# Cross-attention and mixture-of-experts kernel: the store of each turned probability block issued from ScalarE, its loads from SyncE, three block buffers

## What is computed

```python
x = x + xattn(ctx, layernorm(x), mask)      # 16 heads of 64; keys and values: context rows and latent rows
#   q = lat @ Wq;  k, v = [ctx, lat] @ Wk, Wv
#   alphas = softmax(mask(q k^T / 8));  out = (alphas v) @ Wo
x = x + ffn(layernorm(x))                   # 8 experts, the best 2 per token, and a shared expert
#   gates: sigmoid(x gate_w), top 2, normalised; h = silu(x w1) * (x w3); y = (h w2) * gate, summed
```

## Time and profile before

| | before |
|---|---|
| median of 3 runs | 1154.0 us |
| profiled execution, its own time | 1153.85 us |
| span of that execution in the trace | 1152.1 us |
| TensorE busy with matmuls | 1083.4 us (94%) |
| TensorE busy with weight loads | 941.8 us (82%) |
| VectorE busy | 926.4 us (80%) |
| ScalarE busy | 792.1 us (69%) |
| GpSimd busy | 615.2 us (53%) |
| first and last matmul of L860 | 41.2 and 1122.4 us |

### The profile page before, as it was taken

The page is one execution under the profiler, slowest core; times in us unless marked ns, Lnnn a source line. Parts: engine busy times, 40 slices in busy tenths (PEclk is TensorE's granted clock), DMA queues, the critical chain, the costliest instruction groups (busy, mean ns, idle before and its releaser), DMA issues.

```text
span 1152.1 us, 28179 instructions
## 1 busy us (share of the span) xinstructions
PE 1083.4 (94%) x7720; PEld 941.8 (82%) x7720; DVE 926.4 (80%) x4095; ACT 792.1 (69%) x2924; POOL 615.2 (53%) x717
## 2 busy tenths in 40 slices
PE   6899999999999999999999999999999999999976
PEld 6788887888888788888888888888888888888755
DVE  3878887888887788888888888778888788888756
ACT  4887777776777677777776677776777776777631
POOL 5555555555555455555555555555555555554421
PEclk9999999999999999999999999999999999999979
DMA  5455455555455555455555555555455555545531
GB/s 153 141 165 155 152 169 161 163 153 154 150 170 155 162 147 159 145 172 161 171 155 154 154 158 170 168 152 149 137 168 168 168 151 154 155 149 163 157 117 33
DMA packets 248717, 176.81 MB, mean 153 GB/s; under 512 B 29424, under 2 KB 215408, under 8 KB 248560
## 3 DMA queue, kind: packets, MB, share of 16 engines
q1 hardware_dynamic: 247376, 173.96, 50.8%
q10 hardware_dynamic: 1184, 1.05, 0.3%
HBM read 103.35 MB, written 71.56 MB: 152 GB/s over the span
## 4 chain that ended last, share of the span: by engine, by line
SPq 26%; PE 24%; DVE 21%; DMA 11%; issue 11%; ACT 5%; POOL 0%; DVEq 0%; POOLq 0%; ACTq 0%
SPq L335 13%; DMA pT<-probsT_dram 9%; SPq L363 6%; PE bank L860 5%; PE bank L873 4%; PE bank L815 4%; PE bank L817 3%; PE bank L816 3%; SPq L328 3%; DVE logits L671 3%; DVE probsT L686 3%; ACT probs L557 3%; SPq L369 3%; DVE h L704 2%; DVE g_eq L603 2%
## 5 line engine op out<-in xcount | busy, mean ns | idle before, releaser
L453 POOL TENSOR_TENSOR probs<-probs,rdenom 128x512 f32<-128x512 f32 x256 | 266.4, 1041 | 405.0 <-DVE rdenom L680 400.4
L557 ACT ACTIVATE probs<-logits,neg_max 128x128 f32<-128x128 f32 x1024 | 398.7, 396 | 0.9 <-DVE neg_max L671 0.9
L873 PEld LDWEIGHTS bank<-kvT,tT 128*128 128x128 f32 x2048 | 268.8, 192 | 120.3 <-issue 106.8
L860 PE MATMUL bank<-pT,kv_f 128*128 128x512 f32 x512 | 269.3, 607 | 44.2 <-DMA pT<-probsT_dram 43.9
L873 PE MATMUL bank<-kvT,tT 128*128 128x128 f32 x2048 | 270.7, 275 | 0.0
L716 DVE TENSOR_TENSOR cT_lo<-bank,cT_hi 128x512 fp32r<-128x512 f32 x256 | 175.2, 685 | 83.8 <-ACT cT_hi L527 83.7
L671 DVE CUSTOM_DVE_ANT_0 logits<-bank,mask_add 128x128 f32<-128x128 f32 x1024 | 232.6, 282 | 6.1 <-PE bank L873 5.9
L527 ACT CAST cT_hi<-bank 128x512 fp32r<-128x512 f32 x256 | 150.0, 586 | 113.1 <-PE bank L860 112.5
L557 ACT ACTIVATION_READ_ACCUMULATOR probs<-logits,neg_max 128x1 f32 x1024 | 197.6, 193 | 0.0
L512 ACT ACTIVATE h_tanh<-bank 128x256 f32<-128x256 f32 x160 | 61.6, 385 | 180.7 <-PE bank L817 178.3
L686 DVE STREAM_TRANSPOSE probsT<-probs 128x512 f32<-128x512 f32 x256 | 176.0, 688 | 0.7 <-issue 0.5
(11 more groups left out here) (102 smaller groups left out, 1996.4 us busy)
## 6 DMA issues: line engine op xcount, KB each, us to landing
probsT_dram<-probsT SPq DMA_DIRECT2D x256, 256.0 KB, 2.4
pT<-probsT_dram SPq DMA_DIRECT2D x1024, 64.0 KB, 2.2
gates<-gates_dram SPq DMA_DIRECT2D x62, 256.0 KB, 4.2
kv_raw<-in_ctx SPq DMA_DIRECT2D x32, 128.0 KB, 2.8
kv_raw<-in_x SPq DMA_DIRECT2D x32, 128.0 KB, 2.9
mask_raw<-in_mask_BxS_ik SPq DMA_DIRECT2D x32, 128.0 KB, 3.4
x_res<-in_x SPq DMA_DIRECT2D x32, 128.0 KB, 2.7
out<-out_sb SPq DMA_DIRECT2D x32, 128.0 KB, 3.0
```

What stands on the lines that cost most here:

```text
L453: nc.gpsimd.tensor_tensor(by_pair, by_pair, rdenom[n][:, :].unsqueeze(2).unsqueeze(3).broadcast_to([P, PAIRS, P // QUAD, QUAD]), ALU.mult) ...
L557: nc.scalar.activation(probs[c % 4][:, :, r, :], logits[c % 2][:, r, :].rearrange("p (c k) -> p c k", k=QUAD), ACT.Exp, bias=neg_max[c % 2 ...
L860: nc.tensor.matmul(C_ps[c % 2][:, :], kv_f[g % 3][:, kl % 4, :], pT[c % 3][:, :], start=True, stop=True).then_inc(C_in_psum, 1)
L873: last = nc.tensor.matmul(S_ps[c % 2][:, P * r:P * (r + 1)], tT[:, kl % 4, hd:hd + 2, :], kvT[g % 2][:, kl % 4, :], start=True, stop=True)
```

## The change

The store of a block moves from SP to ScalarE, between `tT` and `cT_hi` of the same half (e holds block e - 1, as before). VectorE's transposes go to three buffers `probsT` in turn and no longer wait for the store of two blocks ago but for that of three blocks ago. SP loads block e - 1 in half `e`, at the end of the half and not that of e - 2 at its start. The other transfers get other halves: the gates' loads go from half 6 to half 0 of the next frame, the mask to 1, the residual to 2, the output to 3, the gates' stores two and two to halves 5 and 6, the keys to half 7 of the frame before.

```diff
-        probsT = [sb(f"probsT{n}", [P, PAIRS * P]) for n in range(2)]
+        probsT = [sb(f"probsT{n}", [P, PAIRS * P]) for n in range(3)]
@@ SP
-            def store_probs(s):
...
                 for k in range(HALVES):
                     e = HALVES * i + k
-                    if has_half(e - 1):
-                        store_probs(e - 1)
-                    if has_half(e - 2):
-                        load_probs(e - 2)
-                    if k == 0 and has(j, p, -1, NG - 3):
-                        load_kv(j, p + 2)
+                    if k == 0 and has(j, p, 3, NG + 1):
+                        sp.wait_ge(gates_stored, 64 * (i - 2))
+                        after(sp, h_routed_done, NT * (i - 3))
...
+                    if k == 1 and has(j, p, -1, NG - 3):
                         load_mask(j, p + 2)
-                    if k == 0 and has(j, p, 4, NG + 2):
-                        store_out(i - 1)
-                    if k == 1 and has(j, p, 0, NG - 1):
+                    if k == 2 and has(j, p, 0, NG - 1):
...
+                    if k == 3 and has(j, p, 4, NG + 2):
+                        store_out(i - 1)
-                    if k == 5 and has(j, p, 2, NG):
+                    if k in (5, 6) and has(j, p, 2, NG):
...
-                        for a in range(P // QUAD):
+                        for a in (0, 1) if k == 5 else (2, 3):
...
+                    if k == 7 and has(j, p, -2, NG - 4):
+                        load_kv(j, p + 3)
+                    if has_half(e - 1):
+                        load_probs(e - 1)
@@ ScalarE
+            def store_probs(s):
+                n = s % 3
+                act.wait_ge(probsT_ready, s + 1)
+                after(act, pT_loaded[n], 64 * (s // 3))
+                nc.scalar.dma_start(probsT_dram[n], probsT[n][:, :]).then_inc(probsT_stored[n], 16)
...
+                    if has_half(e - 1):
+                        store_probs(e - 1)
                     if has_half(e - 4):
@@ VectorE
                         dve.wait_ge(probs_ready, c + 1)
-                        if c >= 2:
-                            dve.wait_ge(probsT_stored[(c - 2) % 3], 16 * ((c - 2) // 3 + 1))
-                        nc.vector.transpose(probsT[c % 2][:, :], probs[c % 4][:, :, :, :].rearrange("p c r k -> p (c r k)")
+                        after(dve, probsT_stored[c % 3], 16 * (c // 3))
+                        nc.vector.transpose(probsT[c % 3][:, :], probs[c % 4][:, :, :, :].rearrange("p c r k -> p (c r k)")
```

More of the change, by code:

```diff
@@ L342, in frame @@
                     e = HALVES * i + k
-                    if has_half(e - 1):
-                        store_probs(e - 1)
-                    if has_half(e - 2):
-                        load_probs(e - 2)
-                    if k == 0 and has(j, p, -1, NG - 3):
-                        load_kv(j, p + 2)
+                    if k == 0 and has(j, p, 3, NG + 1):
+                        sp.wait_ge(gates_stored, 64 * (i - 2))
+                        after(sp, h_routed_done, NT * (i - 3))
+                        for a in range(2):
+                            sp.dma_start(gates[FH * a:FH * (a + 1), :, :],
+                                         gates_dram.rearrange("(r a) t -> a r t", a=2)[a, :, :].partition_broadcast(FH)
+                                         ).then_inc(gates_loaded, 16)
+                    if k == 1 and has(j, p, -1, NG - 3):
                         load_mask(j, p + 2)
-                    if k == 0 and has(j, p, 4, NG + 2):
-                        store_out(i - 1)
-                    if k == 1 and has(j, p, 0, NG - 1):
+                    if k == 2 and has(j, p, 0, NG - 1):
                         after(sp, x1_step, 3 * (i - 2) + 1)
```

## The result

The changed kernel takes 1165.82 us (median of 5 runs, 1164.02 to 1167.53) against 1154.26 us for the kernel before (5 runs, 1153.74 to 1157.98). The ratio is 1.0089, with a 95% interval of 1.0066 to 1.0113: slower by 0.9%. The span of the profiled execution is 1164.1 us.

What follows compares the result with a forecast made beforehand. The prediction took TensorE (PE) to bound the kernel: 32.65 + 2.0 = 34.65 us a frame against 34.41, so 7 us over 29 frames, plus 4 for the early frames, on 1153.85: 1165, written as 1164; range 1150 to 1182.

Steps and rivals of the forecast that it cites:

- PE bounds, and needs 32.65 us a frame: Whole kernel: TensorE sets the pace and by itself needs 32.65 us of a frame's 34.41.
- The waits on `pT` go: TensorE at L860: the 43.9 us of waits vanish, giving back up to 1.76 us a frame.
- The slack of 4 us: Loads on SP: the block is back over 4 us ahead of TensorE's start, which pays for a slip.
- The stall in halves 0 and 1: ScalarE's store waits for VectorE's turn ahead of `cT_hi`; TensorE loses 2.0 us a frame at L936 in half 1.
- A frame of 34.65: Full frame: 32.65 us needed plus 2.0 us lost, against 34.41 before.
- The ramp: First two frames, paced by ScalarE: slower halves cost 4 us, with 0 and 7 as ends.
- Zero for the waits of halves 3 to 5: ScalarE in halves 3 to 5: the push from waiting runs out in its idle time at the next tanh, zero.
- Zero for the dealing and for the third buffer: SP's other transfers moved to other halves, and the third `probsT`: each costed at nothing.
- The even trade: Rival: the stall in half 1 only just replaces the waits on `pT`, 1153 to 1157 us; chance 0.21.
- ScalarE's idle time: Rival: ScalarE's idle 31% hides the store, the waits on `pT` go at no cost, 1110 us; chance 0.13.
- The dearer store: Rival: ScalarE's issue takes 0.9 us, the stall in half 1 grows, about 1189 us; chance 0.09.
- The 1135 us that this rule alone would give: Skill's rule: only SP's issue slot is saved, some 0.44 us at each of 42 waits; no chance given.

Runs made afterwards that it cites:

- e1: The changed kernel with ScalarE's store moved to the end of the same half, behind the four exponentials: 1106.83 us.
- e2: The changed kernel with the store at the end of ScalarE's half in halves 0 and 1 only: 1104.66 us.
- e4: The changed kernel with SP's list as in the kernel before except for the stores, loads of block e - 2 first: 1164.91 us.
- e7: The kernel before with three probsT and the store moved from SP to the end of ScalarE's half, SP's list otherwise as before: 1111.18 us.
- e3: The kernel before with only SP's other transfers dealt over the frame's halves; stores, loads and two probsT unchanged: 1119.94 us.
- e8: The changed kernel with the store at the end of ScalarE's half in half 0 only: 1129.12 us.
- e5: The changed kernel with each store issued as two transfers of half the columns: 1245.42 us.
- e6: The changed kernel with two probsT instead of three: 1166.01 us.
- e9: The changed kernel with the store back on SP, just ahead of the loads of the same block: 1478.65 us.

## Why the prediction was right

The forecast was 1164 us, slower, against 1165.82 measured. Step by step:

*PE bounds, and needs 32.65 us a frame.* Right: with the waits out of the way e1 and e2 run at 32.80 and 32.82.

*The waits on `pT` go.* Right in the number: 43.9 us to 2.4. But the step that was to do it, loads that follow their own store, is not what does it: e4 keeps the loads of block e - 2 and waits 3.0 us. It is enough that the store leaves SP's list (9.2 us in e7, without the stall's cover), and e3 gets most of the way with the dealing alone. In detail the loads were less early than I worked out. In half 0 the store issued at 675.60 was followed by loads only at 679.94, a landing of about 4.3 us against the median of 2.4, while the gates' loads, issued from 674.45, were on the way (SP's timeline of the changed kernel):

```profile
674.45 1.25 SPq L341 DMA_DIRECT2D gates<-gates_dram  x2
679.94 1.82 SPq L329 DMA_DIRECT2D pT<-probsT_dram  x4
```

The slack of 4 us, which I had named as the cover, held it. That the gates' loads delay the landing is read from the traces and not tested: in the kernel before, where they stand in half 6, the store with a median landing of 4.3 us is that of half 7.

*The stall in halves 0 and 1.* Right in cause and nearly in size, and in place but for one point. Measured from PE's L860 of half 1 (666.84 in the earlier trace rows, 676.66 after), the first turn ends 1.09 us before it in both kernels. `cT_hi` of half 0 was forecast at -0.60 and came at -0.69; the second turn ended at +3.02 (forecast +3.10), `cT_hi` of half 1 came at +3.42 (+3.59), L936 at +5.21 (+5.44). The stall of 1.79 us is 0.2 smaller than the 2.0, because the store on ScalarE takes 0.33 us and 0.40 from the end of the turn to `cT_hi`, not the 0.49 that I took. SP's median of 0.376 would have been the nearer row; the two transfers at the start of the program, which I chose, are larger ones. PE does not lose it mainly at L936, as I had put it: the wait for `tT` at L815, which I had down as a little, is half of the marked idle time (27.1 us against 25.0). The late exponentials of half 0 hold up both. e8 shows the two waits adding up, and e2 that nothing else costs.

*A frame of 34.65.* Measured 34.65, by a small luck: the stall is 0.2 less, and some 0.15 a frame are lost elsewhere, which e1 shows alone (32.80 against 32.65).

*The ramp: 4 us.* Near in size, but not for the reason given alone. PE's L860 of half 4 in the frame at which the 26 begin starts at 170.71 instead of 163.87, 6.8 us later, of which three frames at 0.24 would be 0.7. Early halves last 55.10 - 51.74 = 3.36 us, against the 2.49 of the earlier trace rows and the 3.45 of the forecast.

```profile
51.74 0.41 ACT L558 ACTIVATE probs<-logits,neg_max 128x128 f32<-128x128 f32 x1
...
55.10 0.41 ACT L558 ACTIVATE probs<-logits,neg_max 128x128 f32<-128x128 f32 x1
```

These slow halves leave PE only 87.91 - 84.86 = 3.05 us late at the L860 ahead of the first stall. That stall alone then costs 7.28 - 4.75 = 2.53 us, as the starts of L860 in half 1 and half 2 show, first before, then after:

```profile
84.86 1.13 PE L860 MATMUL bank<-pT,kv_f 128*128 128x512 f32 x2 [0.47 <-DMA pT<-probsT_dram]
...
89.61 1.02 PE L860 MATMUL bank<-pT,kv_f 128*128 128x512 f32 x2
```

```profile
87.91 1.02 PE L860 MATMUL bank<-pT,kv_f 128*128 128x512 f32 x2
...
95.19 1.02 PE L860 MATMUL bank<-pT,kv_f 128*128 128x512 f32 x2
```

e2 agrees: it keeps the waits of halves 2 to 7, and at the start of the 26 frames it is 170.71 - 163.33 = 7.4 us ahead of the changed kernel and only 163.33 - 161.58 = 1.8 behind e1. So most of the early loss is the stall of halves 0 and 1 in the first full frames, and the 4 us, put on the slow halves, came near partly by luck. Together 6.8 and 26 x 0.24 = 6.1 make 12.9 us; the span grew by 12.0, and the end of the program is shorter by the rest.

*Zero for the waits of halves 3 to 5.* Right for this kernel (e2), but I had not worked out how near the edge it is: half a microsecond more per store, in e5, and PE waits in halves 4 and 6 as well.

*Zero for the dealing and for the third buffer.* Right beside the stall (e4, e6). By itself the dealing was worth some 35 us (e3, a ratio of 0.9689), which the prediction did not say: I had costed it at nothing and put the gain on the earlier loads, although I had the rows of the four bunched issues of half 0 in hand.

*The rivals.* The even trade came within 10 us but the interval excludes it. ScalarE's idle time did not hide the store, since what stands behind it in the list waits with it. The dearer store did not come. The sentence of the Trainium skill, "DMA: Bandwidth & Descriptors", section "Issuing engines are not separate DMA queues", that another engine saves only the time of issuing, is met only in part here: e9 against e1, the same loads with the store on SP or on ScalarE, differ by 372 us, since the issuing queue also stands through the wait that the loads have for the store. The 1135 us that this rule alone would give did not come either (1165.82).

## What to carry to other kernels

A transfer issued from a computing engine costs little time (0.33 us here), but its wait stops everything that stands behind it in that engine's list; so follow what stands behind, engine by engine, until it meets the bound, and put the transfer where its wait is already over. Before giving a queue's work to another engine, look whether its transfers only stand in bunches: spreading them was worth 3% by itself. The best kernels of this study, the change with the store at the end of ScalarE's half in all halves or in halves 0 and 1 alone, take 1106.83 and 1104.66 us, 4.2 to 4.4% below the kernel before.

## What was not expected of the hardware

In e1 the store stands behind the four exponentials of its half, yet it starts ahead of them. ScalarE's timeline of e1, half 0:

```profile
639.99 0.59 ACT L544 COPY kvT<-bank 128x512 f32<-128x512 f32 x1 [0.71 <-PE bank L888]
640.34 0.33 ACTq L493 DMA_DIRECT2D probsT_dram<-probsT  x1
640.48 0.38 ACT L547 CAST latT_hi<-bank 128x256 fp32r<-128x256 f32 x1
640.74 0.42 ACT L556 ACTIVATE probs<-logits,neg_max 128x128 f32<-128x128 f32 x1
```

VectorE's turn had ended at 639.47 + 0.68 = 640.15, and the store starts at 640.34, 0.40 us before the first exponential that precedes it in the list. ScalarE's queue hands its computing instructions on and goes ahead to the transfer. `latT_hi` and the exponential follow `kvT` without a gap, so the transfer costs no computing time here. In 26 full frames the store starts ahead of the last of the four exponentials every time; only in halves 4 and 5, where the turn ends later, does it always start behind the first. The Trainium skill, "Perfetto Trace Analysis", section "Sequencer Loop", says that a sequencer pushes engine instructions into a queue and starts control instructions itself; the trace agrees, with the 0.40 us above. So a place late in the list does not mean a late store, which fits the 4.4 us of waits on `pT` in e1. I had counted on ScalarE's idle time to cover the issue of 0.49 us in the covered halves; where the transfer overtakes, nothing needs to be covered.
